# A second attention with relative terms: two phases made one, by half units

## The chip, the cores and the metric

The kernel runs on one core of a Trainium2 chip (TensorE = PE, VectorE = DVE, ScalarE = ACT, GpSimd = POOL, SyncE = SP). The metric is the time of one execution on the device in microseconds.

## The reference

x [8, 512, 128] goes through four blocks with residuals: attention A with a bias table, a feed-forward block with local attention (depth 2), attention B, and the feed-forward block again. The change touches attention B alone:

```python
dist_idx = pos_l - pos_r + M - 1              # M = 128, negative ones wrap
pos_emb = dist_emb[dist_idx]
rel_q = jnp.einsum('bhld,lrd->bhlr', q, pos_emb)
rel_k = jnp.einsum('bhrd,lrd->bhlr', k, pos_emb)
scores = (scores + rel_q + rel_k) / jnp.sqrt(jnp.asarray(D, scores.dtype))
probs = jax.nn.softmax(scores, axis=-1)
ctx = jnp.einsum('bhqk,bhkd->bhqd', probs, v)
```

It has 16 heads of 8 columns, batch 8, 512 positions. The embedding table has 255 rows, and an index outside it is clipped or wraps, so that far on one side the relative terms repeat a value or a period of 255.

## The kernel before

The kernel is written in phases, with a barrier of all engines between them (`barrier`, numbered). q and k are split into three bf16 parts each, so that a float32 product becomes one bf16 product over 48 rows, the "stack". `split_dram` holds the parts. A unit is 4 heads of one batch element (`QB`), 32 units in all (`UNITS_B`); a unit has 16 tiles (`TILES`), one for each block of 128 rows (`lt`, 4 of them) and head.

**Phase b1** makes the relative terms. For each unit GpSimd loads the stack in twelve pieces (`sync_b1_loads`, L1324). SyncE writes it to `stack_dram` (L1331). TensorE multiplies each 128-column block of the stack with a table of embeddings by distance, `b_e`, over a window of up to 640 distances (L1357, and L1360 for what passes a bank of 512 columns). ScalarE moves the query side (L1378) and VectorE the key side (L1381) from PSUM to `b_stage`, which has two buffers for each side, by `lt % 2`, each for 4 heads. SyncE stores them to `rel_dram` (L1339), whose rows are read back later with a step of one less than a row, and so skewed.

**Phase b2** makes the attention. GpSimd loads the stack again (`c_st`, L1425) and the key side's terms (`c_rk`, L1430), and copies values (L1433). SyncE loads the query side's terms (`c_rq`, L1445). TensorE makes scores (L1456), adds far terms by two products where `lt >= 2` (L1460, L1462) and the key side's terms by transposes into the same bank (L1465). VectorE adds `c_rq` and takes the minimum (L1574), ScalarE takes the exponential (L1539), TensorE transposes the probabilities (L1474), which VectorE and ScalarE move by turns (L1603, L1556). Then come the products with the values (L1485), the scales of the rows (L1495), `move_out` (L1586) and the output product (L1503). Scores run three tiles ahead in four banks.

The order is written out by hand: each engine has its own program in order, and waits on counting semaphores. `hold` is a wait of an engine that issues DMAs. `c_loop` runs the steps of the units; in a step every engine goes over the 16 tiles ("slots").

## Time and profile before

| what | us |
|---|---|
| median of 3 runs (4907.82 to 4912.31) | 4911.35 |
| profiled execution | 4912.15 |
| its span, first to last instruction | 4910.4 |
| PE busy / DVE / ACT / POOL | 3915.1 / 2889.9 / 2635.3 / 1689.6 |
| phase b1, from the first stack load | 2234 to about 3053 |
| phase b2, to the end of its last instructions | about 3059 to 3981 |

### The profile page before, as it was taken

What the parts mean: (1) busy time and instruction counts of PE and PEld (TensorE: products, weight loads), DVE (VectorE), ACT (ScalarE), POOL (GpSimd) and SP (SyncE); (2) the same over time, 40 slices, a digit from 0 to 9 for tenths busy, and PEclk for the clock granted to TensorE, in tenths of its full rate; (3) what the DMA queues carried; (4) which work ended last, traced back from release to release, by engine and by line L of the source; (5) the groups of instructions that cost most, each with busy time, mean ns of one, the idle gap of its engine ahead of it and who ended that gap; (6) DMA issues with size and microseconds to landing.
All of it is one profiled execution on the core that took longest, in us unless ns stands there. A gap on an engine that the chain in (4) does not pass through costs nothing.

```text
span 4910.4 us, 102424 instructions
## 1 busy us (share of the span) xinstructions
PE 3915.1 (80%) x31924; PEld 2380.9 (48%) x31924; DVE 2889.9 (59%) x6305; ACT 2635.3 (54%) x6550; POOL 1689.6 (34%) x1383
## 2 busy tenths in 40 slices
PE   2999999999488888734666565999999945888886
PEld 1555555554255555522222222677777723555554
DVE  2555555555577777543444443566666665777775
ACT  1555555554367777523333333566666624777774
POOL 0000000000588888523222222111111116878774
PEclk9999999999799999965555555999999977999998
DMA  3222222221111111027999999777777711111111
GB/s 118 87 78 78 78 78 80 81 78 53 49 25 23 27 27 23 17 71 293 380 381 385 380 381 369 269 262 260 248 272 250 256 43 52 25 26 25 25 23 32
DMA packets 374686, 701.06 MB, mean 143 GB/s; under 512 B 54180, under 2 KB 161016, under 8 KB 374568
## 3 DMA queue, kind: packets, MB, share of 16 engines
q1 hardware_dynamic: 330536, 565.25, 33.6%
q0 software_dynamic: 44032, 134.30, 7.4%
q8 instruction: 66, 1.08, 0.1%
q14 instruction: 52, 0.43, 0.0%
HBM read 336.53 MB, written 314.64 MB: 133 GB/s over the span
## 4 chain that ended last, share of the span: by engine, by line
PE 51%; DMA 13%; DVE 10%; issue 9%; POOL 7%; ACT 4%; SPq 2%; DVEq 1%; POOLq 0%; ACTq 0%
DMA rel_k<-b_stage_k 12%; PE ps L332 5%; PE ps L1465 5%; PE ps L340 5%; PE ps L351 5%; PE ps L1474 5%; PE ps L1456 3%; PE ps L1485 3%; DVE f_rs L1028 2%; POOL f_rn L758 2%; PE ps L866 2%; DVE f_rc L1025 2%; POOL f_rot L756 2%; PE ps L1357 2%; DVE b_stage_k L1381 2%
## 5 line engine op out<-in xcount | busy, mean ns | idle before, releaser
L1381 DVE COPY b_stage_k<-ps 128x640 f32<-128x640 f32 (+2 forms) x512 | 359.1, 722 | 469.6 <-DMA rel_k<-b_stage_k 410.3
L430 ACT ACTIVATE a_p<-a_s,a_min 128x512 f32<-128x512 f32 x512 | 366.0, 715 | 470.3 <-DVE a_min L474 470.3
L1378 ACT ACTIVATE b_stage_q<-ps 128x640 f32<-128x640 f32 (+2 forms) x512 | 316.0, 624 | 505.4 <-PE ps L1360 388.0
L474 DVE CUSTOM_DVE_ANT_0 a_s<-ps,a_table 128x512 f32<-128x512 f32 x512 | 333.5, 689 | 374.5 <-PE ps L332 371.9
L1539 ACT ACTIVATE c_p<-c_s,c_min 128x512 f32<-128x512 f32 x512 | 370.2, 723 | 290.7 <-PE ps L1474 180.3
L1357 PE MATMUL ps<-b_e,b_st_k 48*128 48x512 bf16 (+1 forms) x512 | 305.9, 597 | 261.1 <-DVE b_stage_k L1381 261.1
L1574 DVE CUSTOM_DVE_ANT_0 c_s<-ps,c_rq 128x512 f32<-128x512 f32 x512 | 352.8, 689 | 200.8 <-PE ps L1465 188.1
L188 POOL COPY y<-ln_rows 128x512 f32 x32 | 19.9, 621 | 1304.8 <-DVE ln_rows L180 1304.8
L949 ACT ACTIVATE f_p<-f_s,f_min 128x128 f32<-128x128 f32 x1024 | 396.3, 390 | 89.1 <-DVE f_min L1014 88.7
L756 POOL TENSOR_TENSOR f_rot<-f_rc,f_rs 128x1024 f32<-128x1024 f32 x128 | 302.9, 2367 | 255.6 <-DVE f_rs L1028 255.3
L758 POOL TENSOR_TENSOR f_rn<-f_ss,f_power 128x16 f32<-128x16 f32 x128 | 373.8, 2920 | 14.9 <-DVE f_ss L1037 1.4
L1357 PE MATMUL ps<-b_e,b_st_q 48*128 48x512 bf16 (+2 forms) x512 | 281.0, 549 | 79.3 <-ACT b_stage_q L1378 52.7
L1474 PE MATMUL ps<-ident,c_p 128*128 128x128 f32 x2048 | 313.3, 276 | 1.1 <-ACT c_p L1539 1.1
L340 PEld LDWEIGHTS ps<-ident,a_p 128*128 128x128 f32 x2048 | 219.6, 141 | 194.8 <-issue 187.6
L1465 PE MATMUL ps<-ident,c_rk 128*128 128x128 f32 x1664 | 296.1, 291 | 0.0
L1324 POOL DMA_DIRECT2D b_st_q<-split_qk x192 | 104.9, 547 | 550.0 <-PE ps L1357 531.6
L332 PE MATMUL ps<-a_kT,a_qT 64*128 64x512 f32 x1024 | 289.0, 641 | 2.0 <-DVE a_min L474 1.2
L340 PE MATMUL ps<-ident,a_p 128*128 128x128 f32 x2048 | 279.8, 279 | 0.4 <-DVE a_pT L498 0.3
L351 PE MATMUL ps<-a_pT,a_v 128*64 128x512 f32 x1024 | 275.5, 617 | 0.0
L1357 PEld LDWEIGHTS ps<-b_e,b_st_k 48*128 48x128 bf16 x512 | 68.0, 133 | 403.2 <-DVE b_stage_k L1381 364.6
L1603 DVE COPY c_pT<-ps 128x512 f32<-128x512 f32 x256 | 176.3, 689 | 139.5 <-PE ps L1474 139.5
L740 POOL TENSOR_TENSOR f_p<-f_p,f_rsum 128x1024 f32<-128x1024 f32 x128 | 242.9, 1898 | 23.2 <-DVE f_rsum L1080 23.2
(171 smaller groups left out, 9194.5 us busy)
## 6 DMA issues: line engine op xcount, KB each, us to landing
rel_q<-b_stage_q SPq DMA_DIRECT2D x64, 1280.0 KB, 7.8
rel_k<-b_stage_k SPq DMA_DIRECT2D x64, 1280.0 KB, 7.7
c_rq<-rel_q SPq DMA_DIRECT2D x64, 1024.0 KB, 7.7
c_rk<-rel_k POOLq DMA_DIRECT2D x64, 1024.0 KB, 11.9
a_table<-skew_bias SPq DMA_DIRECT2D x64, 896.0 KB, 4.6
f_vb<-f_v SPq DMA_DIRECT2D x256, 128.0 KB, 2.4
rel_k<-b_stage_k SPq DMA_DIRECT2D x32, 1024.0 KB, 9.5
rel_q<-b_stage_q SPq DMA_DIRECT2D x32, 1024.0 KB, 5.3
```

Of the source, the lines that this page charges most:

```text
L332: nc.tensor.matmul(ps[:, h, :], a_qT[rows, par, lt * P:(lt + 1) * P], a_kT[rows, par, :], start=True, stop=True).then_inc(a_scored, 1)
L340: last = nc.tensor.transpose(ps[:, 2 + h, rt * P:(rt + 1) * P], a_p[:, lt % 2, h, rt * P:(rt + 1) * P], ident[:, :])
L351: last = nc.tensor.matmul(ps[64 * h:64 * h + 64, 4 + par, :], a_v[:, par, rt, DK * h:DK * h + DK], a_pT[:, par, h, rt, :], start=(rt == 0) ...
L430: nc.scalar.activation(a_p[:, lt % 2, h, :], a_s[:, lt % 2, h, :], ACT.Exp, bias=a_min[:, lt % 2, h:h + 1], scale=-1.0, accum_out=a_sum[:, ...
L756: tt(f_rot[:, :], f_rc[:, :], f_rs[:, :], ALU.add).then_inc(f_rotated, 1)
L758: tt(f_rn[:, :], f_ss[:, 1, :], f_power[:, :], ALU.pow).then_inc(f_rn_ready, 1)
L949: nc.scalar.activation(f_p[:, s2.par, n, :], f_s[:, s2.par, n, :], ACT.Exp, bias=f_min[:, s2.par, n:n + 1], scale=-1.0, accum_out=f_sum[:, ...
L1357: last = nc.tensor.matmul(ps[:, bank, lo:min(hi, 512)], w, b_e[:, n, at + lo:at + min(hi, 512)], start=True, stop=True)
L1381: moves_b1(dve, 1, lambda out, src: nc.vector.tensor_copy(out, src))
L1465: last = nc.tensor.matmul(ps[:, r, rt * P:(rt + 1) * P], c_rk[:, q, rt, h, lt * P:(lt + 1) * P], ident[:, :], start=False, stop=(rt == LT ...
L1474: last = nc.tensor.transpose(ps[:, 2 + r, rt * P:(rt + 1) * P], c_p[:, r, rt * P:(rt + 1) * P], ident[:, :])
L1539: nc.scalar.activation(c_p[:, r, :], c_s[:, r, :], ACT.Exp, bias=c_min[:, r:r + 1], scale=-1.0, accum_out=c_sum[:, q, a:a + 1]).then_inc(c ...
```

## The change

Phases b1 and b2 become one. While the attention of unit s runs, the relative terms of unit s + 1 are made. Everything that is stored and loaded is handled for 2 heads at a time (`HALF`), a half unit: 8 slots, two for each `lt` (`place`). In detail:

- `b_st` has four slots of half a stack, and scores read it directly: `stack_dram` and `c_st` are gone. A load has 2 heads and not 4, so there are twelve for each half unit.
- Each tile has one relative product for each side, of at most 512 columns (`made`: 512, 512, 512, 384 on the query side for lt = 0 to 3, and 384, 512, 512, 512 on the key side). The rest of a window repeats known columns: GpSimd copies it within `b_stage` (`fill`; lt = 0, 1 of the query side, lt = 2, 3 of the key side).
- SyncE stores each `lt` and side by two DMAs of 64 partitions, each with only the columns that its half needs (`store_rel`: 576, 576, 448, 320 columns and the reverse).
- `b_stage` has still two buffers for each side, now for 2 heads. `move_rel` waits for the store of `lt - 2`.
- GpSimd loads `c_rk` for a half unit once all its stores have landed (`load_rk`), then the next half stack (`load_stack`), then makes the four fills.
- A slot of TensorE is now: scores of two tiles ahead, relative products, transposes of probabilities. There are two score banks in place of four.

```diff
-    stack_dram = nc.dram_tensor("stack_qk", [UNITS_B, 2, STACK, QB, SEQ], BF16).ap()
...
+    HALF = QB // 2
+    SLOTS = 4
+    TILES = LT * QB
+    PART = LT * HALF
+    b_st = [sbs("b_st_q", [STACK, SLOTS, HALF, SEQ], BF16), sbs("b_st_k", [STACK, SLOTS, HALF, SEQ], BF16)]
...
+    SCORE_BANKS, PT_BANK, MIX_BANK, REL_BANKS, JOIN_BANK = [0, 1], 2, 4, [5, 6], 7
...
+    def near(n, t):
+        return (P * max(0, t - 1), SEQ) if n == 0 else (0, P * min(LT, t + 2))
+    def place(a):
+        return a // PART, (a % PART) // HALF, a % HALF
+    def made(n, t):
+        lo, hi = near(n, t)
+        return (0, min(512, hi + P - lo)) if n == 0 else (max(0, hi + P - lo - 512), hi + P - lo)
+    PERIOD = DIST_B
+    FILLS = 3
...
+    def fills(n, t):
+        return ((1, 2, 0, 0) if n == 0 else (0, 0, 2, 1))[t]
...
+        def load_stack(u, q, hf):
+            n_slot = 2 * q + hf
+            for n in range(2):
+                for g in range(6):
+                    at = (n * 3 + SPLIT_ORDER[n][g]) * (P * SEQ) + hf * (HALF * DB * SEQ)
+                    src = bass.AP(split_dram.tensor, (u // QB) * (6 * P * SEQ) + (u % QB) * (QB * DB * SEQ) + at,
+                                  [[SEQ, DB], [DB * SEQ, HALF], [1, SEQ]])
+                    pool.dma_start(b_st[n][DB * g:DB * g + DB, n_slot, :, :], src).then_inc(b_st_loaded[n_slot], 16)
...
+        def load_rk(u, hf):
+            for r in range(2):
+                hold(pool, b_rel_stored[1][r], u * 128 + (hf * 64 + 96))
...
+                src = bass.AP(rel_dram[1].tensor, rel_row(u, hf, rt) + (P - 1 + lo),
+                              [[WIN - 1, P], [P * WIN, HALF], [1, hi - lo]])
+                pool.dma_start(c_rk[:, hf, rt, :, 0:hi - lo], src).then_inc(c_rk_loaded[hf], 16)
...
+        def fill(u, hf, n, t):
+            hold(pool, b_rel_moved[n], u * TILES + (hf * PART + t * HALF + HALF + 1))
+            stage = b_stage[n][:, t % 2, :, :]
+            if fills(n, t) == 1:
+                to, at = ((512, WIN), 511) if n == 0 else ((0, P), P)
+                nc.gpsimd.tensor_copy(stage[:, :, to[0]:to[1]], stage[:, :, at:at + 1].broadcast_to([P, HALF, P])
+                                      ).then_inc(b_rel_filled[n], 1)
...
+        def fill_half(u, hf):
+            fill(u, hf, 0, 0)
+            fill(u, hf, 0, 1)
+            fill(u, hf, 1, 2)
+            fill(u, hf, 1, 3)
+        def step(s, q, first, last):
+            hold(pool, c_scored, s * TILES + 32)
+            load_rk(s, 1)
+            if not last:
+                load_stack(s + 1, 1 - q, 1)
+            hold(pool, c_pv, s * LT + 4)
...
+            if not last:
+                fill_half(s + 1, 0)
+                hold(pool, c_scored, s * TILES + (32 + PART))
+                load_rk(s + 1, 0)
+                load_stack((s + 2) % UNITS_B, q, 0)
+                fill_half(s + 1, 1)
...
+        def store_rel(u, hf, lt):
+            for n in range(2):
+                lo, hi = near(n, lt)
+                if fills(n, lt):
+                    hold(sp, b_rel_filled[n], u * (2 * FILLS) + (fills_before(n, hf, lt) + fills(n, lt)))
+                else:
+                    hold(sp, b_rel_moved[n], u * TILES + (hf * PART + lt * HALF + HALF + 1))
+                for g in range(2):
+                    f, w = (1 - g) * (P // 2), hi - lo + P // 2
+                    dst = bass.AP(rel_dram[n].tensor, rel_row(u, hf, lt) + (g * (P // 2) * WIN + lo + f),
+                                  [[WIN, P // 2], [P * WIN, HALF], [1, w]])
+                    sp.dma_start(dst, b_stage[n][g * (P // 2):(g + 1) * (P // 2), lt % 2, :, f:f + w]
+                                 ).then_inc(b_rel_stored[n][lt % 2], 16)
+        def load_rq(u, hf, lt):
+            lo, hi = near(0, lt)
+            hold(sp, b_rel_stored[0][lt % 2], u * 128 + (hf * 64 + 32 * (lt // 2) + 64))
+            src = bass.AP(rel_dram[0].tensor, rel_row(u, hf, lt) + (P - 1 + lo), [[WIN - 1, P], [P * WIN, HALF], [1, hi - lo]])
+            sp.dma_start(c_rq[:, lt, :, lo:hi], src).then_inc(c_rq_loaded[lt], 16)
+        def step(s, q, first, last):
+            for hf in range(2):
+                for lt in range(LT):
+                    if hf == 0 or not last:
+                        hold(sp, c_biased, s * TILES + (hf * PART + lt * HALF + HALF + 24))
+                        load_rq(s + hf, 1 - hf, lt)
+                    if not last:
+                        store_rel(s + 1, hf, lt)
...
+        def relative(u, q, a):
+            hf, lt, h = place(a)
+            if lt == 0 and h == 0:
+                pe.wait_ge(b_st_loaded[2 * q + hf], (u // 2) * 192 + 192)
+            for n in range(2):
+                f, t = made(n, lt)
+                x = EW - WIN - lt * P + near(n, lt)[0]
+                pe.wait_ge(b_rel_moved[n], u * TILES + (a + 1))
+                nc.tensor.matmul(ps[:, REL_BANKS[n], 0:t - f], b_st[n][:, 2 * q + hf, h, lt * P:(lt + 1) * P],
+                                 b_e[:, n, x + f:x + t], start=True, stop=True).then_inc(b_rel_full[n], 1)
...
+            hf, lt, h = place(a)
+            r, sl = SCORE_BANKS[a % 2], 2 * q + hf
+            far = near(0, lt)[0]
+            if lt == 0 and h == 0:
+                pe.wait_ge(c_rk_loaded[hf], u * 64 + 64)
+            pe.wait_ge(c_biased, u * TILES + (a + 23))
+            queries = b_st[0][:, sl, h, lt * P:(lt + 1) * P]
+            nc.tensor.matmul(ps[:, r, :], queries, b_st[1][:, sl, h, :], start=True, stop=False)
+            if far > 0:
+                nc.tensor.matmul(ps[:, r, 0:far], queries, b_e[:, 0, 0:1].broadcast_to([STACK, far]), start=False, stop=False)
+                nc.tensor.matmul(ps[:, r, 0:far], b_e[:, 1, EW - 2:EW - 1].broadcast_to([STACK, P]), b_st[1][:, sl, h, 0:far],
+                                 start=False, stop=False)
+            for rt in range(far // P, LT):
+                last = nc.tensor.matmul(ps[:, r, rt * P:(rt + 1) * P], c_rk[:, hf, rt, h, lt * P:(lt + 1) * P],
                                         ident[:, :], start=False, stop=(rt == LT - 1), is_transpose=True)
...
+                if a + AHEAD < TILES:
+                    scores(s, q, a + AHEAD)
+                elif not last:
+                    scores(s + 1, 1 - q, a + AHEAD - TILES)
+                if not last:
+                    relative(s + 1, 1 - q, a)
+                transpose_probs(s, a)
+                if a == 1 and not first:
                     mix_values(s - 1, 1 - q, LT - 1)
+                if a == 3 and not first:
                     row_scales(s - 1, 1 - q)
-                if lt == 2 and not first:
+                if a == 9 and not first:
                     out_project(s - 1)
+                if a in (11, 13, 15):
+                    mix_values(s, q, (a - 11) // 2)
...
+    def move_rel(eng, n, u, a, move):
+        hf, lt, h = place(a)
+        f, t = made(n, lt)
+        if h == 0:
+            eng.wait_ge(b_rel_stored[n][lt % 2], u * 128 + (hf * 64 + 32 * (lt // 2) + 32))
+        eng.wait_ge(b_rel_full[n], u * TILES + (a + 1))
+        move(b_stage[n][:, lt % 2, h, f:t], ps[:, REL_BANKS[n], 0:t - f]).then_inc(b_rel_moved[n], 1)
```

On GpSimd, in the program of phase b2 before, one unit reads as follows (c_st: the stack, c_rk: the key side's terms):

```order
L1425 ISA [waits c_scored]
L1425 DMA c_st<-stack_qk 48x2x2048
L1430 ISA
L1430 REGISTER_ALU
L1430 DMA c_rk<-rel_k 128x4x256
L1430 ISA
L1430 DMA c_rk<-rel_k 128x4x384
L1430 ISA
L1430 DMA c_rk<-rel_k 128x4x512
L1430 ISA
L1430 DMA c_rk<-rel_k 128x4x512
L83 ISA
```

The stack and `c_rk` of a unit come by five DMAs, with no wait for a store. In the changed program, in the first step, the same engine has this between two loads of `c_rk` (b_st_q, b_st_k: the half stack; b_stage: the staging buffers):

```order
L1391 DMA c_rk<-rel_k 128x2x512 x2
L1382 DMA b_st_q<-split_qk 8x2x512 x6
L1382 DMA b_st_k<-split_qk 8x2x512 x6
L1424 COPY c_v<-b_v_all 128x4x8 [waits c_pv]
L1424 COPY c_v<-b_v_all 128x4x8 x3
L1399 COPY b_stage_q<-b_stage_q 128x2x128 [waits b_relq_moved]
L1403 COPY b_stage_q<-b_stage_q 128x2x126 [waits b_relq_moved]
L1405 COPY b_stage_q<-b_stage_q 128x2x2
L1408 COPY b_stage_k<-b_stage_k 128x2x127 [waits b_relk_moved]
L1409 COPY b_stage_k<-b_stage_k 128x2
L1399 COPY b_stage_k<-b_stage_k 128x2x128 [waits b_relk_moved]
L1391 DMA c_rk<-rel_k 128x2x256 [waits c_scored,b_relk_stored0,b_relk_stored1]
```

Behind the `c_rk` loads of a half unit now stand twelve stack loads, then the value copies, and only then the copies of `fill`; the next `c_rk` loads wait for `b_relk_stored`, all stores of the half unit.

On SyncE, the changed program has around the first slots of a step:

```order
L1463 DMA c_rq<-rel_q 128x2x512 [waits c_biased,b_relq_stored0]
L1456 DMA rel_q<-b_stage_q 64x2x576 [waits b_relq_filled]
L1456 DMA rel_q<-b_stage_q 64x2x576
L1456 DMA rel_k<-b_stage_k 64x2x320 [waits b_relk_moved]
L1456 DMA rel_k<-b_stage_k 64x2x320
L1463 DMA c_rq<-rel_q 128x2x512 [waits c_biased,b_relq_stored1]
L1456 DMA rel_q<-b_stage_q 64x2x576 [waits b_relq_filled]
L1456 DMA rel_q<-b_stage_q 64x2x576
L1456 DMA rel_k<-b_stage_k 64x2x448 [waits b_relk_moved]
L1456 DMA rel_k<-b_stage_k 64x2x448
```

The store of the query side waits for `b_relq_filled`, and the store of the key side, which needs no fill at these `lt`, comes after it in the queue.

On TensorE, one tile in phase b2 before:

```order
L1456 MATMUL ps<-c_st 128x512 [waits c_biased]
L1465 MATMUL ps<-ident,c_rk 128x128 x4
L1474 MATMUL ps<-ident,c_p 128x128 [waits c_pT1_emptied,c_exped]
L1474 MATMUL ps<-ident,c_p 128x128 x3
L1456 MATMUL ps<-c_st 128x512 [waits c_biased]
```

and now, at the first tile of a half unit (c_rk_loaded1 is the landing of its `c_rk`):

```order
L1504 MATMUL ps<-b_st_k,b_st_q 128x512 [waits c_biased,c_rk_loaded1]
L1510 MATMUL ps<-ident,c_rk 128x128 x4
L1493 MATMUL ps<-b_e,b_st_q 128x384 [waits b_relq_moved]
L1493 MATMUL ps<-b_e,b_st_k 128x512 [waits b_relk_moved]
L1519 MATMUL ps<-ident,c_p 128x128 [waits c_pT0_emptied,c_exped]
L1519 MATMUL ps<-ident,c_p 128x128 x3
L1504 MATMUL ps<-b_st_k,b_st_q 128x512 [waits c_biased]
```

The relative products stand between the scores and the transposes of the probabilities, and each waits for the move of the one before it on its side.

## Rows read from the trace of the kernel before

**Rows 1.** Windows: us, busy us (x count) of each engine, granted clock, DMA share, GB/s

```profile
2300.00:3000.00 700.00, 424.03 (x1547) 183.80 (x1546) 309.23 (x442) 271.10 (x440) 176.65 (x324) 0.50 1.02 382
3200.00:3900.00 700.00, 700.00 (x7913) 494.62 (x7911) 439.51 (x1080) 437.29 (x1029) 108.31 (x225) 1.00 0.74 258
2234.00:3981.00 1747.00, 1390.33 (x11902) 847.23 (x11903) 919.57 (x1887) 875.51 (x1825) 350.32 (x675) 0.75 0.86 310
```

**Rows 2.** Waits in 2244:3052: us in total, times, longest

```profile
DVE b_stage_k L1381 <- DMA rel_k<-b_stage_k: 410.3, 126, 4.9
```

**Rows 3.** DMA queues, total: 2244:3052, and below 3052:3980

```profile
DMA packets 150091, 307.96 MB, mean 381 GB/s; under 512 B 13984, under 2 KB 46293, under 8 KB 150089
...
DMA packets 100392, 233.02 MB, mean 251 GB/s; under 512 B 4650, under 2 KB 37877, under 8 KB 100377
```

**Rows 4.** Timeline of PE, 2632.2:2632.8: start us, us, what

```profile
2632.31 0.63 PE L1357 MATMUL ps<-b_e,b_st_k 48*128 48x512 bf16 x1
...
2632.74 0.31 PE L1360 MATMUL ps<-b_e,b_st_k 48*128 48x128 bf16 x1
```

**Rows 5.** Timeline of POOL, 3300:3335

```profile
3303.75 0.58 POOL L1425 DMA_DIRECT2D c_st<-stack_qk  x1 [16.01 <-PE ps L1465]
...
3304.57 3.01 POOL L1430 DMA_DIRECT2D c_rk<-rel_k  x4 [0.24 <-issue]
...
3314.92 0.75 POOL L1433 COPY c_v<-b_v_all 128x32 f32 x4 [7.34 <-PE ps L1485]
...
3331.71 0.58 POOL L1425 DMA_DIRECT2D c_st<-stack_qk  x1 [16.04 <-PE ps L1465]
```

**Rows 6.** Page, costliest groups: busy us, mean ns, idle before

```profile
L188 POOL COPY y<-ln_rows 128x512 f32 x32 | 19.9, 621 | 1304.8 <-DVE ln_rows L180 1304.8
```

**Rows 7.** DMA issues in 2244:2262, the first of the phase: KB each, median us to landing

```profile
rel_q<-b_stage_q SPq DMA_DIRECT2D x2, 1280.0 KB, 6.0
...
stack_qk<-b_st_q SPq DMA_DIRECT2D x1, 192.0 KB, 2.7
```

**Rows 8.** DMA issues in 2244:3052

```profile
rel_k<-b_stage_k SPq DMA_DIRECT2D x64, 1280.0 KB, 7.7
```

**Rows 9.** Timeline of POOL, 2640:2655

```profile
2645.86 3.57 POOL L1324 DMA_DIRECT2D b_st_q<-split_qk  x6 [17.65 <-PE ps L1357]
...
2649.53 3.57 POOL L1324 DMA_DIRECT2D b_st_k<-split_qk  x6
```

**Rows 10.** Groups by form in 3052:3985: busy us, mean ns, idle before

```profile
L1574 DVE CUSTOM_DVE_ANT_0 c_s<-ps,c_rq 128x512 f32<-128x512 f32 x512 | 352.8, 689 | 200.8 <-PE ps L1465 188.1 <-issue 4.6 <-ACT c_p L1539 2.7
...
L1574 DVE DVE_READ_ACCUMULATOR2_ANT c_min<- 128x1 f32 x512 | 42.1, 82 | 0.0
...
L1603 DVE COPY c_pT<-ps 128x512 f32<-128x512 f32 x256 | 176.3, 689 | 139.5 <-PE ps L1474 139.5
```

**Rows 11.** Chain of waits in 3080:3092: start us, us, what

```profile
3080.71 0.60 PE ps L1456
...
3086.37 0.54 PE ps L1456
3086.91 1.04 PE ps L1465 x4
3087.95 0.85 PE ps L1474 x4
```

**Rows 12.** Windows at the start of phase two, columns as rows 1

```profile
3088.00:3090.00 2.00, 2.00 (x9) 1.23 (x8) 0.70 (x2) 1.15 (x3) 0.00 (x0) 0.50 1.02 418
3090.00:3092.00 2.00, 2.00 (x15) 1.45 (x13) 1.44 (x4) 0.92 (x4) 0.00 (x0) 0.98 1.02 318
```

More of the change, by code:

```diff
@@ L1388, in program @@
+    b_stage = [sbs("b_stage_q", [P, 2, HALF, WIN]), sbs("b_stage_k", [P, 2, HALF, WIN])]
+    c_rk = sbs("c_rk", [P, 2, LT, HALF, SEQ])
+    c_rq = sbs("c_rq", [P, LT, HALF, SEQ])
     c_v = sbs("c_v", [P, 2, LT, QB, 32])
@@ new lines, in pool_b1, with sync_b1 @@
+        load_stack(0, 0, 0)
+        load_stack(0, 0, 1)
+        load_stack(1, 1, 0)
+        fill_half(0, 0)
+        fill_half(0, 1)
+        load_rk(0, 0)
+        c_loop(pool, step)
+        pool.wait_ge(b_st_loaded[0], 192 * (UNITS_B // 2 + 1))
+        pool.wait_ge(b_st_loaded[2], 192 * (UNITS_B // 2))
+    def sync_b1(sp):
+        def store_rel(u, hf, lt):
[3 more added lines that the diff above has]
+                    hold(sp, b_rel_filled[n], u * (2 * FILLS) + (fills_before(n, hf, lt) + fills(n, lt)))
+                else:
+                    hold(sp, b_rel_moved[n], u * TILES + (hf * PART + lt * HALF + HALF + 1))
[18 more added lines that the diff above has]
+                        store_rel(s + 1, hf, lt)
+        sp.wait_ge(c_pad, LT - 1)
+        for hf in range(2):
+            for lt in range(LT):
+                store_rel(0, hf, lt)
+        for lt in range(LT):
+            load_rq(0, 0, lt)
+        c_loop(sp, step)
@@ L1552, in step @@
                     exps(s + 1, 1 - q, 0)
+                if not last:
+                    move_rel(act, 0, s + 1, a, move)
                 if a % 2 == 1:
@@ L1558, in step @@
                     move_scale(s - 1)
+        for a in range(TILES):
+            move_rel(act, 0, 0, a, move)
         exps(0, 0, 0)
@@ L1599, in step @@
                     bias_and_min(s + 1, 1 - q, a + 2 - TILES)
+                if not last:
+                    move_rel(dve, 1, s + 1, a, move)
                 if a % 2 == 0:
@@ L1605, in step @@
                     invert_sums(s - 1, 1 - q)
-                if a == 5 and not first:
+                if a == 6 and not first:
                     move_out(s - 1, 1 - q)
@@ L1609, in step @@
                     add_to_y(s - 1)
+        dve.wait_ge(c_pad, LT - 1)
+        for a in range(TILES):
+            move_rel(dve, 1, 0, a, move)
         bias_and_min(0, 0, 0)
@@ L1769, in _ @@
         barrier(dve, 7)
-        vector_b2(dve)
-        barrier(dve, 8)
         dve.sem_inc(residual_added, 1)
@@ L1774, in _ @@
         vector_ln(dve, 4)
+        barrier(dve, 8)
+        vector_ffn(dve, 1)
         barrier(dve, 9)
-        vector_ffn(dve, 1)
-        barrier(dve, 10)
         add_block(dve)
```

231 lines of the change are left out of this document (64 added, 167 removed).

## The prediction

> **What bounds the kernel now.** I read first the windows [rows 1], which cut the second attention into its two phases. In the first one TensorE is busy 424 of 700 us at a granted clock of 0.50 (1.2 GHz), and the DMA engines are busy all the time at 382 GB/s; VectorE's longest wait there is for a store of its own staging buffer, 410.3 us in 126 waits [rows 2]. So transfers bound phase one. In the second phase TensorE is busy 700 of 700 us at clock 1.00 (2.4 GHz) and the DMA share is 0.74. So TensorE bounds phase two. Both together, with the barrier between them, last 1747 us (2234 to 3981) of the profiled execution's 4912.15 us. Nothing outside is touched, so the question is what takes the place of these 1747 us.
>
> **What the merge could win.** Bytes first. Phase one moved 307.96 MB, phase two 233.02 MB [rows 3]. A unit's relative terms were stored in 4 x 2176 columns on each side; a half unit now stores 1920 columns for 2 heads (576, 576, 448, 320), so 285 MB become 252 MB. The stack's store and second load (12.6 MB each) go. Left are 252 + 12.6 MB at 382 GB/s, 692 us, and 218 MB of loads at 258/0.74 = 349 GB/s, 625 us: 1317 us, or 20.6 us for each of 64 half units. TensorE next. Phase two's cadence is 3331.71 - 3303.75 = 27.96 us for 16 tiles [rows 5], 1.75 us a tile at full clock. The two relative products of a tile have on average 2 x 480 columns; at the low clock products of 512 columns start 0.43 us apart [rows 4], so they add 0.80 us low or 0.40 us full. A tile is then 2.15 us, a half unit 17.2 us at full clock and 34.4 us at the low one. Were nothing else in the way, some 21 to 22 us for each half unit would be left of today's 1747/64 = 27.3.
>
> **What stands in the way: the order on GpSimd.** Let time run from the moment when VectorE has moved the last relative tile of a half unit (slot 7 or 15). From there every step waits for the one before it:
>
> 1. GpSimd fills 128 columns of 2 heads. A copy of 512 columns takes 621 ns [rows 6], the small value copies 0.75/4 = 0.19 us [rows 5]; between these I take 0.45 us.
> 2. SyncE stores lt = 3 of both sides, 896 KB. Alone, 1280 KB landed after 6.0 us and 192 KB after 2.7 us [rows 7], on the line between them 4.9 us. Bounds: 2.7, and 7.7 of the saturated phase [rows 8]. I take 4.9, as the queue has gaps now (20.6 of some 30 us busy).
> 3. Only then may GpSimd issue the four loads of `c_rk`: four took 3.01 us with 512 rows each [rows 5]; with 256 rows 2.8 us (2.2 to 3.0).
> 4. Behind them in the same queue are the twelve loads of the next half stack. Twelve took 3.57 + 3.57 us and a gap, 7.2 us [rows 9]. A load has half the rows now, but between 32 rows (0.60) and 512 rows (0.75) there is little to save: 7.2 us. There are twice as many of them, since each brings two heads and not four.
> 5. Four value copies, in every second half unit: 0.4 us on average.
> 6. Only now comes the fill for lt = 0 of the query side: 0.45 us. Its tiles were ready in slot 1, long before.
> 7. SyncE stores lt = 0 of both sides (query side first, so the key side is queued behind that fill), 896 KB: 4.9 us.
> 8. Six hand-overs between engines and queues at about 0.15 us (one gap between two loads on GpSimd shows 0.24 [rows 5]): 0.9 us.
>
> That is 22.0 us. Until then ScalarE and VectorE stand at `move_rel` of slot 4, which needs the staging buffer of lt = 0, and with them TensorE stops at the relative product of slot 5. The buffer is the reason: there are two for each side, by lt % 2.
>
> 9. The tail, from the move of slot 4 to that of slot 7. VectorE needs 0.69 for that move and then three bias passes at 0.69 + 0.08, three moves and two copies of probabilities at 0.69 [rows 10], and in every second half `move_out`: 6.1 us. TensorE at the low clock needs more: scores 0.54 + 1.04 = 1.58 us, four transposes 0.85 [rows 11], relative products of two tiles of a slot 0.86 (1024 columns) and 0.75 (896). From relative 5 to relative 7: 0.86 + 0.85 + 1.58 + 0.75 + 0.85 + 1.58 + 0.75 = 7.2, and the last move 0.7. So 8.6 us at the low clock, 6.8 at the full one.
>
> Which clock? Between one last move and the next stop TensorE has about five and a half slots, some 12 us of full-clock work, in an interval of 22.7 us: it idles for 6 to 10 us in every half unit. In the trace phase two's first product starts at 3080.71 [rows 11], the engine then runs without a break, and it was given the full clock only in the window from 3090 on [rows 12]; in phase one, with breaks, it stayed at 0.50 [rows 1]. I take the low clock for the tail and so 22.0 + 8.6 = **30.6 us for a half unit**. The rest hides in it: transfers (20.6), the loads of `c_rk` (needed only at slot 14 or 6, some 6 slots after step 3), the score banks cut from four to two, ScalarE's exponentials. If the GpSimd part went, the transfers would be late next.
>
> **The sum.** 31 units have their relative terms made beside the unit before: 62 half units x 30.6 = 1897 us. Ahead of them: memsets 2.4, 36 stack loads 22, the stores of unit 0 in two halves and the first load of `c_rk`, about 60 us. Behind them a last unit without relative terms, 16 x 1.75 and its start and end, about 35 us. Together 1992 us against 1747: **245 us more**, 5157 us in a profiled execution and 5156 against the median of 4911.35 us, which is 0.8 us under the profiled one. The change breaks even at (1747 - 95)/62 = 26.6 us for a half unit.
>
> A page speaks on steps 2 and 7. The row shows 1280 KB alone in 6.0 us [rows 7]. The Trainium skill (DMA: Bandwidth & Descriptors, section Anatomy of one DMA) has a DMA cost 2.0 us plus its bytes at 436 GB/s; by that both stores would take an estimated 4.1 us each and the total would be about 5057 us, still slower. By that rule the 1280 KB would have been 5.0, so the row speaks for the larger price.
>
> **The rivals.**
> *A: the waits are shorter.* Steps 2 and 7 at 3.3 us each instead of 4.9, since the queue may be empty then, and TensorE keeps its clock over the stop, so that VectorE's 6.8 bounds the tail: 18.8 + 6.8 = 25.6 us, 62 x 25.6 + 95 = 1682, so 4847 us, faster. It decides at 26.6 us. For it: 192 KB in 2.7 us. Against it: those 6.0 us for 1280 KB, and the idle 6 to 10 us. Chance 0.14.
> *B: the GpSimd queue isn't in the way* (the fills are ahead of need because the loads are issued in time), and transfers bound: 22.5 us, 62 x 22.5 + 95 = 1490, 4654 us. The order on GpSimd speaks against it. Chance 0.08.
> *C: the clock stays low and TensorE is the bound:* 34.4 us, 62 x 34.4 + 95 = 2228, 5392 us. For it: phase one stayed at 0.50 for 700 us at 61% busy [rows 1]. Against it: at that cadence the engine would have no breaks, and without breaks it was given the full clock [rows 12]. Chance 0.15. The Trainium skill (TensorE: Matmul & The Clock Gate, Part 1) says that the throttled state is the default and that sustained activity releases it. Rows 12 agree; for a stage with a stop in every half unit it speaks for C's low clock and against A.
>
> **How the numbers follow.** My forecast has 0.63; its own range is 27.5 to 33.5 us a half unit, 4964 to 5336 us. The range for 8 in 10 goes on to A (its upper half) and to C: 4860 to 5400. A and B are faster by more than 0.2% (which is about what a measurement of this kernel can tell): 0.21 with their edges. Within 0.2% needs 26.4 to 26.8 us: 0.03. Slower: 0.76.
>
> **What would show it.** Right if, in the changed profile, VectorE's and ScalarE's longest waits are at `move_rel` for the stores of `rel_q` and `rel_k`, once in a half unit; if GpSimd's twelve stack loads stand between its four `c_rk` loads and the first fill, and these loads start some 5 to 6 us after the last fill; if the DMA share is near 0.7, TensorE is idle about a fourth to a third of the stage and its clock falls once in a half unit. Wrong if the cadence of the `c_rk` loads is under 26.6 us, if TensorE waits for `c_rk` rather than for the moves, or if the DMA share is near 1.

## The result and the profile after

| | before | after |
|---|---|---|
| median, four runs of each | 4910.84 us | 5295.7 us (5286.6 to 5303.21) |
| ratio to before, 95% interval | | 1.0784 (1.0765 to 1.0803) |
| span of the profiled execution | 4910.4 us | 5301.5 us |
| the stage of the change | 2234 to 3981, 1747 us | 2234 to 4371, 2137 us |

The kernel is 7.8% slower. The stage is 390 us longer, so all of the loss lies in it. By the prediction's own form, (2137 - 95)/62 = 32.9 us for a half unit, where 30.6 were forecast.

The page of the kernel after, three lines of its sections 2 and 3 (40 slices of 132.5 us each; the stage is in slices 17 to 33):

```profile
PEclk9999999997999998656767777676766775999999
DMA  3222222221111111177777777777777761111111
...
DMA packets 396580, 642.67 MB, mean 121 GB/s; under 512 B 78532, under 2 KB 219160, under 8 KB 396456
```

58 MB less are moved than before (701.06), the clock is five to seven tenths over the whole stage, and the DMA share is 0.7: neither transfers nor TensorE are at their limit. The windows say the same (us, busy us (x count) of each engine, granted clock, DMA share, GB/s; [rows 1] are those of before):

```profile
2400.00:4200.00 1800.00, 1392.79 (x9500) 743.95 (x9499) 731.65 (x1608) 716.28 (x1553) 639.77 (x1312) 0.70 0.75 228
2234.00:4371.00 2137.00, 1638.96 (x11100) 871.77 (x11104) 859.70 (x1886) 842.67 (x1824) 757.75 (x1551) 0.69 0.74 226
```

TensorE stands still for 23% of the time, and works at a mean clock of 0.70. The waits of 2400 to 4200, 55 half units (engine, line, what it waited for: us in total, times, longest); the last line is of SyncE's queue:

```profile
ACT b_stage_q L1594 <- DMA rel_q<-b_stage_q: 508.7, 80, 13.7
DVE b_stage_k L1631 <- DMA rel_k<-b_stage_k: 483.6, 83, 13.1
...
PE ps L1493 <- ACT b_stage_q L1594: 383.8, 55, 11.7
...
SPq L84 <- POOL b_stage_q L1399: 758.1, 55, 16.1
```

ScalarE and VectorE wait at `move_rel` for the stores (before it was 410.3 us in phase b1 alone [rows 2]), TensorE once in each half unit for them. The last line has the root: SyncE waits once in each half unit for the fill of lt = 0 on GpSimd, 13.8 us in the mean (758.1/55). What GpSimd does meanwhile, its timeline from 3304 to 3362 (start us, us, what, idle before and releaser):

```profile
3309.05 0.40 POOL L1399 COPY b_stage_k<-b_stage_k 128x256 f32<-128x256 f32 x1 [6.03 <-DVE b_stage_k L1631]
3318.19 2.92 POOL L1391 DMA_DIRECT2D c_rk<-rel_k  x4 [8.75 <-issue]
3321.11 3.41 POOL L1382 DMA_DIRECT2D b_st_q<-split_qk  x6
3324.60 3.58 POOL L1382 DMA_DIRECT2D b_st_k<-split_qk  x6
3328.19 0.41 POOL L1399 COPY b_stage_q<-b_stage_q 128x256 f32<-128x256 f32 x1
...
3343.96 0.40 POOL L1399 COPY b_stage_k<-b_stage_k 128x256 f32<-128x256 f32 x1 [5.86 <-DVE b_stage_k L1631]
3349.85 2.92 POOL L1391 DMA_DIRECT2D c_rk<-rel_k  x4 [5.50 <-DMA rel_k<-b_stage_k]
```

The order is the forecast one: last fill, a gap, four loads of `c_rk`, twelve stack loads, and only then the fill that frees the query side's store. The first gap, 8.75 us, is the longest of its kind: from the start of the last fill to the first load of `c_rk` it is 9.14 us here and 6.7 in the mean of 54 half units. The chain names 4.44 of it as the landing of the stores and 2.48 as issue time with no cause that the profile shows. The chain of waits through the same round (start us, us, what):

```profile
3308.49 0.62 SPq L1456
3309.30 0.61 SPq L1456
3310.16 0.60 SPq L1456
3310.94 4.44 DMA rel_k<-b_stage_k
3315.68 2.48 issue
...
3331.18 3.02 DMA rel_k<-b_stage_k
3334.31 0.70 DVE b_stage_k L1631
...
3336.71 1.86 PE ps L1531 x32
```

Each time one `lt` is stored, four issues of 0.6 us stand one behind the other on SyncE, three of them on the path ahead of the landing. The windows of four us from 3324 show the stop and the clock:

```profile
3324.00:3328.00 4.00, 4.00 (x43) 2.53 (x43) 0.70 (x2) 1.50 (x4) 3.67 (x7) 0.66 0.40 143
3328.00:3332.00 4.00, 1.82 (x11) 0.82 (x9) 0.70 (x2) 0.00 (x0) 1.05 (x4) 1.00 0.49 112
3332.00:3336.00 4.00, 1.55 (x4) 0.61 (x5) 1.69 (x3) 1.89 (x4) 0.00 (x0) 0.70 0.89 236
3336.00:3340.00 4.00, 4.00 (x41) 2.51 (x39) 1.40 (x4) 1.30 (x3) 0.52 (x2) 0.50 1.00 330
3340.00:3344.00 4.00, 4.00 (x46) 2.33 (x49) 3.20 (x7) 2.42 (x6) 0.04 (x1) 0.95 0.95 325
```

TensorE stops for 4.26 us ahead of the relative product of 3334.08, its clock falls from 1.00 to 0.50 before it starts again, it works through most of the tail at the low clock, and has the full one again shortly after 3340. That is a short case: in windows of 1 us from 2400 to 4000 there are 48 stretches at the low clock, about one for each half unit, of 3 to 34 us, and together they are 946 of the 1600 us.

### The profile page after: what moved, and what is told of

The parts are those of the page before. It is cut to its first block, busy times and chain, and to the rows that moved or that the text cites. A ratio compares the mean times of both kernels' runs of the same rounds, so it can differ in the third digit from the quotient of the medians.

```text
span 5301.5 us, 105816 instructions
## 1 busy us (share of the span) xinstructions
PE 4163.6 (79%) x31156; PEld 2404.4 (45%) x31156; DVE 2831.7 (53%) x6305; ACT 2602.0 (49%) x6550; POOL 2096.7 (40%) x2259
## 4 chain that ended last, share of the span: by engine, by line
PE 38%; issue 15%; POOL 14%; DVE 9%; DMA 9%; SPq 7%; ACT 4%; POOLq 1%; DVEq 1%; ACTq 0%
DMA rel_k<-b_stage_k 8%; SPq L1456 6%; PE ps L332 5%; PE ps L340 5%; PE ps L351 5%; POOL b_st_q L1382 3%; PE ps L1510 2%; PE ps L1519 2%; POOL b_st_k L1382 2%; PE ps L1493 2%; DVE f_rs L1028 2%; POOL f_rn L758 2%; PE ps L866 2%; POOL c_rk L1391 2%; DVE f_rc L1025 2%
## 5 line engine op out<-in xcount | busy, mean ns | idle before, releaser
L1594 ACT ACTIVATE b_stage_q<-ps 128x512 f32<-128x512 f32 (+1 forms) x512 | 292.0, 570 | 982.4 <-DMA rel_q<-b_stage_q 578.1
L1631 DVE COPY b_stage_k<-ps 128x512 f32<-128x512 f32 (+1 forms) x512 | 335.4, 655 | 583.1 <-DMA rel_k<-b_stage_k 553.1
L1493 PE MATMUL ps<-b_e,b_st_q 48*128 48x512 bf16 (+1 forms) x512 | 240.9, 471 | 460.8 <-ACT b_stage_q L1594 434.8
L1519 PE MATMUL ps<-ident,c_p 128*128 128x128 f32 x2048 | 444.3, 354 | 0.2 <-ACT c_p L1600 0.2
L1519 PEld LDWEIGHTS ps<-ident,c_p 128*128 128x128 f32 x2048 | 285.6, 176 | 263.1 <-issue 261.1
L1510 PE MATMUL ps<-ident,c_rk 128*128 128x128 f32 x1664 | 380.6, 356 | 0.0
L1391 POOL DMA_DIRECT2D c_rk<-rel_k x256 | 187.0, 733 | 395.2 <-DMA rel_k<-b_stage_k 202.3
L1493 PEld LDWEIGHTS ps<-b_e,b_st_q 48*128 48x128 bf16 x512 | 49.3, 96 | 584.4 <-ACT b_stage_q L1594 454.7
L1510 PEld LDWEIGHTS ps<-ident,c_rk 128*128 128x128 f32 x1664 | 228.0, 175 | 140.0 <-issue 129.2
L1493 PE MATMUL ps<-b_e,b_st_k 48*128 48x512 bf16 (+1 forms) x512 | 244.5, 478 | 33.8 <-DVE b_stage_k L1631 33.8
```

The lines of the kernel that those rows point to most:

```text
L1493: nc.tensor.matmul(ps[:, REL_BANKS[n], 0:t - f], b_st[n][:, 2 * q + hf, h, lt * P:(lt + 1) * P], b_e[:, n, x + f:x + t], start=True, stop= ...
L1510: last = nc.tensor.matmul(ps[:, r, rt * P:(rt + 1) * P], c_rk[:, hf, rt, h, lt * P:(lt + 1) * P], ident[:, :], start=False, stop=(rt == LT ...
L1519: last = nc.tensor.transpose(ps[:, PT_BANK + r, rt * P:(rt + 1) * P], c_p[:, r, rt * P:(rt + 1) * P], ident[:, :])
L1631: return nc.vector.tensor_copy(out, src)
```

## The experiments

**Theory:** the order on GpSimd holds the fill of lt = 0 back, and this wait with the stores behind it makes the half unit (steps 2 to 7). **Rivals:** the transfers or TensorE at the low clock set the time, and the order hides beside them (B, C). The first four kernels ran on one chip, with before at 4918.11 us. Differences in us below are between medians; before itself lay between 4910.77 and 4918.11 us beside the various groups of kernels, so a difference across groups, and every one to after in experiments 1 to 4, is good to some 10 us only.

**1. The stack loads behind the first fills.** The diff's core:

```diff
             load_rk(s, 1)
-            if not last:
-                load_stack(s + 1, 1 - q, 1)
...
-                fill_half(s + 1, 0)
+                fill_half(s + 1, 0, (0, 1))
+                load_stack(s + 1, 1 - q, 1)
+                fill_half(s + 1, 0, (2, 3))
                 hold(pool, c_scored, s * TILES + (32 + PART))
                 load_rk(s + 1, 0)
+                fill_half(s + 1, 1, (0, 1))
                 load_stack((s + 2) % UNITS_B, q, 0)
-                fill_half(s + 1, 1)
+                fill_half(s + 1, 1, (2, 3))
```

> The twelve stack loads of a half unit are issued behind the fills of lt = 0, 1 and no longer ahead of them; nothing else moves. Theory (the chain goes through GpSimd's queue to the fill, the store and the staging buffer): the 7.0 us of the twelve loads leave the chain, a half unit falls from 32.7 to about 25.5 us, and the total to 4790 to 4900 us (62 x 7.0 = 434 us less than 5296). Rival 1 (TensorE at its low clock is the bound, 34 us a half unit): no change, 5250 to 5300 us. Rival 2 (SyncE's issues and the transfers bound): under 100 us gained, over 5190 us.

Measured: 4965.99 us, 1.0101 of before (1.0084 to 1.0118). A change of order alone, with the same instructions, takes 330 us off, 5.3 us for each half unit. It missed its range on the small side: the twelve loads are worth 7.0 us on the queue (3.41 + 3.58 and a gap), but a part comes back. The chain of waits of this kernel, and below it the first product of TensorE behind its stop:

```profile
3305.21 3.40 DMA rel_k<-b_stage_k
...
3312.36 0.42 POOL b_stage_q L1399
...
3320.26 6.21 DMA rel_k<-b_stage_k
```

```profile
3327.33 0.60 PE L1492 MATMUL ps<-b_e,b_st_k 48*128 48x512 bf16 x1 [1.25 <-DVE b_stage_k L1630]
```

The fill now comes 2.9 us after the start of the `c_rk` loads and not 10, but behind it SyncE issues the stores of lt = 0 and lt = 1 and a load between them, 7.2 us from 3313.02 to 3320.26, and the last of these lands after 6.21 us, where after had 3.02 to 4.44. In this round the stop has moved from slot 4 to slot 6, whose buffers wait for the stores of lt = 1.

**2. As 1, and the fill of the query side's lt = 0 ahead of the loads of `c_rk` too.** In both places:

```diff
+            if not last:
+                fill(s + 1, 0, 0, 0)
             hold(pool, c_scored, s * TILES + 32)
             load_rk(s, 1)
...
+                fill(s + 1, 1, 0, 0)
                 hold(pool, c_scored, s * TILES + (32 + PART))
                 load_rk(s + 1, 0)
+                fill(s + 1, 1, 0, 1)
```

> As the run before, and besides the fill of lt = 0 on the query side is made ahead of the four loads of c_rk, which wait for stores. Theory: now the store of lt = 0 no longer waits for the landing of the last stores nor for the c_rk loads; what is left is the chain move, fill, store, c_rk load, scores, and TensorE: 21.5 to 24 us for a half unit, a total of 4640 to 4780 us, below the kernel before. If instead the landing of c_rk is late for slot 14 or 6, 4800 us and more, with TensorE waiting for c_rk. Rival 1 (low clock bounds): 5250 to 5300.

Measured: 4910.98 us, 0.9995 of before (0.9981 to 1.0008). That is 385 us under after, and it was expected to be more than 500. The theory holds and its sum doesn't: with the order mended the next limit comes soon. The expectation also named a case of 4800 us and more with TensorE waiting for `c_rk`; that wait is 33.6 us in 2400 to 3800, and the one for the move of the key side is 89.7. Windows of 2400 to 3800 and, below, two of four us at and behind a stop:

```profile
2400.00:3800.00 1400.00, 1274.31 (x9264) 690.84 (x9264) 714.24 (x1574) 707.02 (x1519) 625.01 (x1277) 0.78 0.89 287
...
3312.00:3316.00 4.00, 1.96 (x6) 0.91 (x6) 2.50 (x5) 0.58 (x2) 3.40 (x8) 0.62 1.05 403
3316.00:3320.00 4.00, 4.00 (x14) 2.02 (x14) 1.99 (x5) 2.79 (x7) 0.49 (x2) 0.50 1.06 395
```

and the chain of waits, with TensorE's own first product behind the stop below it:

```profile
3305.71 7.47 DMA rel_k<-b_stage_k
...
3314.04 0.60 PE ps L1495
...
3338.50 1.87 PE ps L1533 x32
...
3341.81 0.59 PE ps L1521 x4
```

```profile
3314.04 0.60 PE L1495 MATMUL ps<-b_e,b_st_k 48*128 48x512 bf16 x1 [2.37 <-DVE b_stage_k L1633]
```

TensorE is busy 91% of the time, at a clock of 0.78. On the path stands a landing of 7.47 us, at a DMA share of 0.98 to 1.05 from 3308 to 3316, but TensorE itself is idle for only 2.37 us of it. It then works without a break from 3314.04, at the low clock until about 3340.3: four transposes take 1.04 us before and 0.59 from 3341.81. So rival C's low clock is on the path now, though not throughout, and so are B's full DMA engines at this place.

**3. Each stack load issued twice**, the second into a buffer that nothing reads:

```diff
                     pool.dma_start(b_st[n][DB * g:DB * g + DB, n_slot, :, :], src).then_inc(b_st_loaded[n_slot], 16)
+                    pool.dma_start(b_scr[DB * g:DB * g + DB, n, n_slot, :, :], src).then_inc(b_scr_loaded[n_slot], 16)
```

> The changed kernel with each stack load issued twice, the second time into a buffer that nobody reads: twelve more issues of 0.58 us on GpSimd in each half unit, 12.6 MB more of transfers. Theory: 7 us more on the chain, 39.7 us for a half unit, 5296 + 62 x 7.0 = 5730 us (5680 to 5780). Rivals 1 and 2: GpSimd's queue has slack, 5296 to 5340 us.

Measured, in two runs: 5779.25 us, 1.1749 (1.1725 to 1.1772): 484 us more, 7.8 us for each of 62 half units, at the upper end of its range. Every microsecond of issue on GpSimd counts, though the DMA share falls to 0.63. Were transfers or TensorE the bound, the longer queue would have hidden at first. Both rivals fall as the bound of the kernel after:

```profile
2400.00:4400.00 2000.00, 1251.63 (x8588) 667.97 (x8587) 663.34 (x1461) 651.53 (x1413) 921.85 (x1797) 0.67 0.63 193
```

**4. One store of 128 partitions for each lt and side** in place of two of 64. It moves all columns that either half needs, 285 MB and not 252:

```diff
-                for g in range(2):
-                    f, w = (1 - g) * (P // 2), hi - lo + P // 2
...
+                w = hi - lo + P
+                dst = bass.AP(rel_dram[n].tensor, rel_row(u, hf, lt) + lo, [[WIN, P], [P * WIN, HALF], [1, w]])
+                sp.dma_start(dst, b_stage[n][:, lt % 2, :, 0:w]).then_inc(b_rel_stored[n][lt % 2], 16)
```

> The changed kernel with one store of 128 partitions for each lt and side in place of two of 64: 128 more columns in place of 64, so 285 MB and not 252 MB of stores, and half the issues on SyncE (0.70 us each in the trace of the changed kernel, where nine in a row take some 8 us at lt = 0 and 1). Theory with SyncE's issues as a term of the chain: the first store pair and the last one each come about 1.4 us earlier, minus 0.2 us for the bytes: 1.5 to 2.5 us a half unit, 5140 to 5210 us. Rival 2 in its form of bytes (transfers bound): slower by 33 MB at 382 GB/s, 5380 us. If issues don't matter: 5290 to 5310 us.

Measured: 5109.99 us, 1.0387 (1.037 to 1.0405), 186 us under after, 3.0 us for each half unit, more than the 1.5 to 2.5 expected, although 33 MB more are moved. SyncE's timeline, first of after, below of this kernel:

```profile
3328.84 1.41 SPq L1456 DMA_DIRECT2D rel_q<-b_stage_q  x2
3330.49 1.54 SPq L1456 DMA_DIRECT2D rel_k<-b_stage_k  x2
```

```profile
3326.41 0.38 SPq L1454 DMA_DIRECT2D rel_q<-b_stage_q  x1
3327.05 0.37 SPq L1454 DMA_DIRECT2D rel_k<-b_stage_k  x1
```

Both sides of an `lt` are issued 1.0 us after the first start, and 3.2 us with halves. The path of a half unit has two such places (steps 2 and 7), so 4.4 us could go, of which 3.0 did. The Trainium skill (DMA: Bandwidth & Descriptors, Rules for kernel authors) advises against two transfers to the halves of the partitions, since they share the same engines, and for one of 128. The result agrees; what it costs here is issue time on the queue.

The next four kernels, with before at 4910.77 us: the measures together, the buffers alone, and a filler.

**5. Order of 2 and store of 4.** No new lines.

> The new order on GpSimd (fill of lt = 0 ahead of the c_rk loads, stack loads behind the fills) together with one store of 128 partitions for each lt and side. In the run of the new order alone the chain still had a stop of 7.5 us at a store, and TensorE then ran at the low clock for some 27 us. Theory (a chain whose terms add): SyncE's saved issues take 1.5 to 3 us from that stop, 4720 to 4830 us, and the granted clock of the stage rises from 0.78 to over 0.85. If the bytes count now, since the DMA share was 0.89: 4900 to 4960 us.

Measured: 4837.97 us, 0.9853 (0.9836 to 0.9869). The two gains are 385 and 186 us alone and 458 together. The time is just outside its range, and the clock of the stage rose to 0.81 (2400 to 3700), not over 0.85. What waits has changed:

```profile
PE ps L1503 <- DMA c_rk<-rel_k: 115.5, 41, 5.7
```

It is now the scores of a half unit's first tile that wait, for `c_rk`, which the prediction named as the sign of another limit.

**6. A staging buffer for each lt and side,** order and stores as in after:

```diff
-    b_stage = [sbs("b_stage_q", [P, 2, HALF, WIN]), sbs("b_stage_k", [P, 2, HALF, WIN])]
+    b_stage = [[sbs(f"b_stage_q{t}", [P, HALF, (640, 640, 512, 384)[t]]) for t in range(LT)],
+               [sbs(f"b_stage_k{t}", [P, HALF, (384, 512, 640, 640)[t]]) for t in range(LT)]]
```

> The changed kernel with its own order on GpSimd and its two stores, but one staging buffer for each lt and side instead of two by lt % 2 (each as wide as its lt needs). Theory: ScalarE and VectorE no longer stop at slot 4, TensorE's tail leaves the chain; what stays is the round c_rk loads 2.9, stack loads 7.0, four fills 2, SyncE's issues of a half unit some 12, landing 3.5, so 27 to 28 us for a half unit, 4930 to 5060 us. If the buffers aren't what links the fill to TensorE: 5280 to 5310 us.

Measured: 5275.87 us, 1.0745 (1.0727 to 1.0763), 20 us under after: a clear miss, instructive for it. The stop of TensorE behind the move of slot 4 goes (it waits for `c_rk` instead, 216.4 us in 40 half units of 2400 to 3700), and the round on the queues stays. The chain of this kernel, then GpSimd's timeline:

```profile
3339.93 0.63 SPq L1457
...
3356.07 0.62 SPq L1457
3356.88 3.32 DMA rel_k<-b_stage_k
```

```profile
3328.70 2.92 POOL L1392 DMA_DIRECT2D c_rk<-rel_k  x4 [15.81 <-PE ps L1511]
...
3361.03 2.93 POOL L1392 DMA_DIRECT2D c_rk<-rel_k  x4 [16.12 <-DMA rel_k<-b_stage_k]
```

Between the two `c_rk` loads lie 32.3 us: 10.3 of loads and value copies on GpSimd, a fill, then SyncE's issues behind each other from 3339.93 to the last store of the key side at 3356.88 = 17.0 us (I had reckoned 12; all twenty take 18.4, until 3358.35), and the landing of 3.32. All stores now come late in one run, since the first still waits for the first fill. The buffer was the place where the wait showed; its cause was the order and the number of issues.

**7. Order, store and buffers together.**

> All three: the new order on GpSimd, one store for each lt and side, four staging buffers. Theory: no stop is left in the chain, TensorE (17.2 us at the full clock) and the transfers (285 + 13 MB at 382 GB/s and 218 MB at 349 GB/s, 1404 us or 21.9 us a half unit) are the bounds: 4640 to 4740 us, DMA share over 0.95. If TensorE gets no full clock for most of the time, 4800 to 4950 us.

Measured: 4830.12 us, 0.9835 (0.9819 to 0.9851). With the others in place, the buffers give 8 us over kernel 5, small, but the four runs of each don't overlap. Of the two expected cases it is the second, with the full clock only part of the time (0.80 in 2400 to 3600).

**8. A filler against the fall of the clock:** on after, ahead of the relative products of slots 5 and 13, 24 products of 512 columns into a bank that is overwritten later.

```diff
+                if not last and a % PART == 5:
+                    c_pT_slot[1].wait_free(pe, s * 8 + a // 2)
+                    for k in range(24):
+                        nc.tensor.matmul(ps[:, PT_BANK + 1, :], b_st[0][:, 2 * q + a // PART, 0, 0:P],
+                                         b_e[:, 0, 0:512], start=True, stop=True)
```

> The changed kernel with 24 extra products of 512 columns in each half unit, in slots 5 and 13 ahead of the relative products, that is where TensorE stops for the stores; they write a bank of which the next transposes overwrite every column. They take 5.2 us at the full clock and 10.3 us at the low one, in a stop that is 5 to 7 us long in the trace. Theory that the low clock in the tail and behind it is a term of the chain (some 2 us a half unit): if the filler keeps the clock up, the granted clock of the stage goes from 0.70 to over 0.85 and the time falls by 60 to 150 us, to 5150 to 5240 us. If it doesn't keep it up, the fillers are in the way, 5350 us and more. If the clock is no term: 5280 to 5310 us at a higher clock.

Measured: 5343.38 us, 1.0871 (1.0845 to 1.0897), 48 us slower than after, close to the case that was expected if it fails (5350 us and more). It didn't do what it was for. The filler and the next product of TensorE, and two windows, the first of 1 us:

```profile
3327.84 5.95 PE L1562 MATMUL ps<-b_e,b_st_q 48*128 48x512 bf16 x24
3335.63 0.60 PE L1493 MATMUL ps<-b_e,b_st_q 48*128 48x512 bf16 x1 [1.84 <-ACT b_stage_q L1599]
```

```profile
3332.00:3333.00 1.00, 1.00 (x5) 0.39 (x4) 0.00 (x0) 0.00 (x0) 0.00 (x0) 0.73 0.97 194
...
3344.00:3348.00 4.00, 4.00 (x14) 2.01 (x14) 1.82 (x6) 2.20 (x5) 0.40 (x1) 0.50 0.93 304
```

The clock fell inside the filler, with TensorE busy all the time, and not in the stop of 1.84 us behind it; it stayed low until about 3352.5, some 20 us. This is no single case: in 13 of the 39 fillers from 2400 to 3700 the clock falls from 1.00 to 0.50 while the filler runs (it then takes 5.9 to 8.1 us in place of 5.35). At 2656.27 and at 3097.89 it did so with no stop behind the filler at all. The mean clock rose from 0.70 to 0.74; how much of this is the filler itself isn't separated. What the clock alone costs in the kernel after is left open by it.

The last four kernels, with before at 4913.19 us, part bytes from issues and look for the next limit.

**9. Buffers and one store, order of after** (6 and 4).

> Four staging buffers as in the run with buffers alone, GpSimd's old order, and one store for each lt and side. In the trace of the run with buffers alone the round was c_rk loads, stack loads, first fill 10.4 us, SyncE's 20 issues one behind the other 18.4 us, landing 3.3 us. Theory (that round is the bound there, and a store of 64 partitions costs SyncE 0.61 us and a gap where one of 128 costs 0.37): SyncE's 12 issues take some 9 us, a half unit 23 to 25 us, 4760 to 4900 us, about 400 us under the run with buffers alone, although GpSimd's order is the old one. If the low clock or the bytes are what bounds: over 5100 us.

Measured: 5066.5 us, 1.0305 (1.0283 to 1.0327): direction right, size missed. It is 209 us under kernel 6, so with the run of issues on the path each of them counts: from SyncE's first issue to the last store it is 9.5 us (3326.80 to 3336.30) in place of 17.0, close to the 9 expected. What the expectation lacked is behind them: a landing of 7.24 us, at a DMA share of 1.05 from 3336 to 3344, and the same unexplained issue gap, here of 2.50 us:

```profile
3336.30 7.24 DMA rel_k<-b_stage_k
...
3343.76 2.50 issue
```

**10. Order and buffers, two half stores.**

> New order on GpSimd and four staging buffers, but the two stores of 64 partitions: beside the run with all three it has 33 MB less to transfer and 20 instead of 12 issues on SyncE in a half unit. Theory: SyncE's queue (17 to 18 us of issues in a half unit of 24) is now close to the bound and late at the last store: 4840 to 4940 us, no better than 4830. If bytes are the bound of the run with all three: 4750 us.

Measured: 4875.8 us, 0.9913 (0.989 to 0.9937), within its range, 46 us over kernel 7, which differs in the store alone.

**11. As 7, with `c_rk` loaded in parts,** each waiting for its own store only and placed between the fills:

```diff
-        def load_rk(u, hf):
-            for r in range(LT):
-                hold(pool, b_rel_stored[1][r], u * 32 + (hf * 16 + 32))
-            for rt in range(LT):
+        def load_rk(u, hf, parts=(0, 1, 2, 3)):
+            for rt in parts:
+                hold(pool, b_rel_stored[1][rt], u * 32 + (hf * 16 + 32))
...
-                load_rk(s + 1, 0)
+                load_rk(s + 1, 0, (0, 1))
+                fill_half(s + 1, 0, (3,))
+                load_rk(s + 1, 0, (2,))
+                fill(s + 1, 1, 0, 0)
+                load_rk(s + 1, 0, (3,))
```

> The run with all three (new order, one store, four buffers, 4830 us), and c_rk loaded part by part: the load of each rt waits only for its own store, rt = 0 and 1 behind the fill of slot 13 or 5, rt = 2 behind the fill of the last slot, rt = 3 last. In that run TensorE stopped some 5 us for c_rk, whose four loads of 1.7 MB landed 8.5 us after the last issue at a DMA share of 1.0, and then ran about 15 us at the low clock. Theory: only one load is left behind the last store, the stop goes in most half units and the clock with it: 4640 to 4740 us, granted clock of the stage over 0.9. If the transfers are saturated over the whole half unit: 4790 to 4830 us.

Measured: 4754.64 us, 0.9671 (0.9649 to 0.9694): 3.3% faster than before and 541 us under after. It beats both kernels, but misses its range of 4640 to 4740 us, and the clock that was expected over 0.9 is 0.84:

```profile
2400.00:3600.00 1200.00, 1117.38 (x8807) 612.44 (x8806) 672.53 (x1490) 669.88 (x1439) 592.41 (x1201) 0.84 0.96 337
```

The DMA share is 0.96 and TensorE is busy 93% of the time. It still waits for `c_rk`, 69.6 us in 27 half units of this window. Rival B's bound, the transfers, is nearly reached as a mean of the stage only here, at 337 GB/s and with 285 MB of stores.

**12. As 11, with the two half stores,** 33 MB less.

> As the run before with the changed kernel's two stores of 64 partitions: 33 MB less, 8 issues more in a half unit. If bytes bound: faster than the run before by up to 80 us. If SyncE's issues do: slower by 50 to 150 us. Theory: SyncE's 17 to 18 us of issues come to lie between the last fill and the last store, so the second.

Measured: 4822.38 us, 0.9809 (0.9788 to 0.983), 68 us over kernel 11, as the case for issues had it. Even where transfers are nearly saturated, twelve issues and more bytes beat twenty issues and fewer.

## Why the prediction was right

The sign, the place and the mechanism are as forecast: 5156 was said, 5295.7 measured, in the upper part of the range (4964 to 5336). The sum was 140 us short, 2.3 us for each half unit. The means of 54 half units between 2400 and 4200 say where (the forecast with its hand-overs in brackets): last move to first `c_rk` load, steps 1 and 2, 7.6 us (5.7); from there to the fill of the query side, steps 3 to 5, 10.3 (10.7); fill to the move of slot 4, steps 6 and 7, 6.2 (5.7); tail 8.9 (8.6); together 33.0 (30.6). By the steps, for the round from the last move at 3308.26 to the next at 3343.07, with 34.8 us a long one:

- **Step 1** (0.45) lies beside the query side's store, which SyncE issues first.
- **Step 2** (4.9) took 6.9: 2.5 from the first issue to the last, and a landing of 4.44. **Step 7** (4.9) took 5.4: 2.3 and 3.02. In the next round they took 5.8 and 5.3. This is the term that was too small. It took a landing by bytes [rows 7] and left out that four issues of 0.6 us stand in front, one behind the other. Experiment 4, which takes two of the four out at both places, gained 186 us. The landings alone were shorter than 4.9; the 6.0 us of [rows 7] weren't of a store alone, since SyncE issued a key side store of 768 KB 0.57 us behind it, which took 6.7 us, and the line between the two rows gives 4.8. So a landing priced too high covered a part of the term left out, and that the sum came so close is partly luck.
- The gap of 2.8 us from that landing to the first `c_rk` load was in step 8 with 0.15. Of three rounds in a row it stands in this one alone; in the two behind it GpSimd starts 0.75 and 0.85 us after the landing, still several times the 0.15. In 10 of the 54 half units the last fill and the first load of `c_rk` are 8 us or more apart. Its cause is open.
- **Step 3** took 2.92 (2.8 said), **step 4** 7.0 (7.2), **step 6** 0.41 (0.45). Experiments 1 and 3 confirm step 4 as on the path: 5.3 us back when it moves, 7.8 us more when it doubles.
- **Step 9** took 8.8 (8.6). It left out the product with the values, 1.86 us (`mix_values`, L1531), and the clock came back earlier than said, from about 3340.3 on. The two nearly cancel here, by luck. Every second half unit has no such product in its tail, and there it takes 8.4 us; in the others it is 7.9 to 10.3, the longest where the clock stays low throughout.

The low clock was rightly put on the tail, but it lasts much longer than the tail, 946 of 1600 us; most of that lies beside the round on the queues. The rule that the prediction cites for the clock, sustained activity releases it, isn't enough here: kernel 2 worked for 26 us without a break before it had the full clock, and in kernel 8 the clock fell amid a run of products. TensorE was idle for 23% of the time, a little under the fourth to a third that was forecast. Rival C's cadence of 34.4 us isn't far from the 32.9, but its reason, TensorE without breaks, is contradicted by its 23% of idle time and by 385 us for an order. Its mechanism returned once the order was mended (experiment 2). Of rival A's conditions the landing of 3.3 us came near, but with the issues ahead of it the waits weren't shorter, and the full clock through the tail didn't come; B's saturated transfers came for short stretches in kernels 2 and 9, and as a mean of the stage, 0.96, only in kernel 11. By the Trainium skill's figures for a DMA (DMA: Bandwidth & Descriptors, Anatomy of one DMA) the total was 5057, further from the truth than the sum by rows. The section gives its fit for DMAs that GpSimd issues, and these stores go out on SyncE; even so its 4.1 us suit the landings of 3.02 and 4.44, and what fails is the same missing term, the issues.

Where did the expected gain of the merge go? The order took 385 us and the half stores some 70 more (kernels 2 and 5 in steps), the two staging buffers 8, and waiting with all of `c_rk` for all stores another 75 to 80 (7 to 11). What is left between kernel 11 and the prediction's "some 21 to 22 us for each half unit" is by its windows and waits the nearly saturated transfers, the late `c_rk` and the low clock; they weren't separated.

## What to carry to other kernels

In a queue that runs in order, put the small operation that frees a buffer ahead of the long run of issues that nobody needs soon: here that alone, without an instruction more or less, was worth 385 us of 5296. Count issues as well as bytes on every queue of the path, since stores cut in two to save 12% of their bytes cost more than they saved in each of the five pairs that differ in it, by 46 to 209 us. When a cycle is broken at one link, price the cycle that is left before expecting the gain: the staging buffers, where the wait showed, were worth 20 us.
